# Wide pick for two tiles, and rows for five tiles fetched by SyncE, in a DLRM tower on one core

## The reference

```
e = jnp.stack([tbl_0[ids[:, 0]], tbl_1[ids[:, 1]], ..., tbl_26[ids[:, 26]]], axis=1)   # (2048, 27, 128)
interactions = jnp.einsum('bfd,bgd->bfg', e, e)
flat_interactions = interactions[:, _TRIU_I, _TRIU_J]                                   # (2048, 351)
z = jnp.concatenate([e.reshape(B, -1), flat_interactions], axis=1)
h = jnp.concatenate([z, dense_ctx], axis=1)                                             # (2048, 3823)
h = jnp.maximum(h @ W_top1 + b_top1, 0.0)                                               # 512
h = jnp.maximum(h @ W_top2 + b_top2, 0.0)                                               # 256
y = h @ W_top3                                                                          # (2048, 1)
```

## Time and profile before

| | us |
|---|---|
| median of 3 runs | 558.83 (558.7 to 559.23) |
| the profiled execution | 559.26 |
| its span, first to last instruction | 557.5 |
| outside the span | 1.76 |
| TensorE matmuls busy | 522.9 (94%) |
| GpSimd busy | 399.2 (72%) |
| ScalarE busy | 255.6 (46%) |
| VectorE busy | 243.9 (44%) |

### The profile page before, as it was taken

One profiled execution on the slowest core, in us unless ns is written; L12 is line 12 of the kernel. 1 busy time (PEld: TensorE's weight loads), 2 busy tenths in 40 slices (PEclk: granted clock), 3 DMA queues, 4 the chain that ended last, 5 costly groups with the idle time before them and its releaser, 6 DMA issues.

```text
span 557.5 us, 12647 instructions
## 1 busy us (share of the span) xinstructions
PE 522.9 (94%) x4420; PEld 429.9 (77%) x4420; DVE 243.9 (44%) x491; ACT 255.6 (46%) x488; POOL 399.2 (72%) x419
## 2 busy tenths in 40 slices
PE   0769889999999999999999999999999999999996
PEld 0547668878788788888888888888888888888884
DVE  3563533436254352534435253443525344352544
ACT  3674545353353535435353543535354353533542
POOL 6777777777777777777777777777777777777600
PEclk9998999999999999999999999999999999999999
DMA  6784321212112112211212121221212122111100
GB/s 171 257 256 130 110 54 57 57 54 60 53 56 59 55 54 56 60 54 57 59 54 59 54 59 54 58 61 55 59 54 59 53 57 60 55 53 54 53 2 1
DMA packets 27041, 38.80 MB, mean 70 GB/s; under 512 B 12455, under 2 KB 16504, under 8 KB 26978
## 3 DMA queue, kind: packets, MB, share of 16 engines
q0 software_dynamic: 13280, 27.22, 17.6%
q1 hardware_dynamic: 13698, 10.77, 6.7%
HBM read 37.96 MB, written 0.01 MB: 68 GB/s over the span
## 4 chain that ended last, share of the span: by engine, by line
PE 72%; POOL 17%; issue 6%; DMA 3%; ACT 1%; DVE 0%; DVEq 0%; ACTq 0%; POOLq 0%
POOL gathered L320 17%; PE p_hid L668 17%; PE p_hid L670 16%; PE p_hid L669 16%; PE p_prod L735 10%; PE p_group L638 7%; DMA gathered<-tbl_dram,idx 3%; PE p_group L626 1%; PE p_group L625 1%; PE p_hid_t L700 1%; PE p_group L655 1%; DMA idx<-ids_dram 0%; ACT emb L351 0%; PE p_hid L735 0%; PE p_hid_t L735 0%
## 5 line engine op out<-in xcount | busy, mean ns | idle before, releaser
L320 POOL DMA_INDIRECT gathered<-tbl_dram,idx x415 | 399.0, 961 | 128.5 <-issue 118.9
L668 PE MATMUL p_hid<-w_high,emb_high 128*128 128x512 f32 x432 | 183.6, 425 | 0.0
L670 PE MATMUL p_hid<-w_high,emb_low 128*128 128x512 f32 x432 | 171.0, 396 | 0.0
L669 PE MATMUL p_hid<-w_low,emb_high 128*128 128x512 f32 x432 | 169.7, 393 | 0.0
L469 DVE TENSOR_TENSOR emb_low<-p_group,emb_high 128x384 fp32r<-128x384 f32 x144 | 80.3, 558 | 195.3 <-ACT emb L351 194.8
L344 ACT ACTIVATE emb_high<-p_group 128x384 fp32r<-128x384 f32 x144 | 70.7, 491 | 161.3 <-PE p_group L638 145.3
L351 ACT ACTIVATE emb<-p_group 128x384 f32<-128x384 f32 x144 | 125.4, 871 | 0.0
L638 PE MATMUL p_group<-identity,gathered 128*128 128x128 f32 x415 | 73.2, 284 | 28.8 <-DMA gathered<-tbl_dram,idx 28.8
L670 PEld LDWEIGHTS p_hid<-w_high,emb_low 128*128 128x128 f32 x432 | 81.7, 189 | 19.4
L669 PEld LDWEIGHTS p_hid<-w_low,emb_high 128*128 128x128 f32 x432 | 82.5, 191 | 12.9
L668 PEld LDWEIGHTS p_hid<-w_high,emb_high 128*128 128x128 f32 x432 | 82.1, 190 | 12.4
(11 more groups left out here) (73 smaller groups left out, 358.6 us busy)
## 6 DMA issues: line engine op xcount, KB each, us to landing
fetched<-tbl_dram SPq DMA_DIRECT2D x512, 0.5 KB
w_stage<-w_dense_dram SPq DMA_DIRECT2D x27, 256.0 KB, 3.6
gathered<-tbl_dram,idx POOLq DMA_INDIRECT x415, 2.5
pick_ids<-ids_rows_dram SPq DMA_DIRECT2D x13, 62.5 KB
w_stage<-w_pairs_dram SPq DMA_DIRECT2D x3, 252.0 KB
w_stage<-w_dram SPq DMA_DIRECT2D x2, 256.0 KB, 3.8
w_stage<-tbl_dram SPq DMA_DIRECT2D x2, 250.0 KB
ctx_sb<-ctx_rows_dram SPq DMA_DIRECT2D x16, 13.5 KB
```

What stands on the lines that cost most here:

```text
L320: pool.indirect_dma_start(gathered[:, slot, k, :], None, tables[f], bass.IndirectOffsetOnAxis(ap=idx[:, t, f:f + 1], axis=0),).then_inc(gr ...
L668: nc.tensor.matmul(dst, high, w_high, start=start, stop=False)
L669: nc.tensor.matmul(dst, high, w_low, start=False, stop=False)
L670: return nc.tensor.matmul(dst, low, w_high, start=False, stop=stop)
```

## The change

The pick is made for two tiles at once. In the even tiles 2 to 12 VectorE makes the 0/1 matrices for the tile's own 128 samples behind `layer3` in the entry of group 4, and those of the next tile's samples in the entry of group 5, into one tensor with 256 columns. TensorE makes 16 matmuls of 256 columns, which fill the third and the fourth place of the bank. ScalarE copies the fourth place to `next_high` and to the next tile's `emb`, VectorE subtracts to `next_low`, and the next tile takes feature 26 from there. In tile 14, as in tiles 0, 1 and 15, it is gathered.

SyncE fetches feature 25 for tiles 4, 6, 9, 11 and 14. It takes the row numbers from SBUF, 32 at a time, and starts when the last weight's load is issued; it no longer does anything else in between. The loads of the context and of the pick's row numbers go out from ScalarE's queue, in the entries of groups 6 and 7 of the tile before. There are five staging slots for the weights. The room that the gathers' descriptors get is 2048 bytes per partition instead of 4096. `y` has 16 columns instead of 128, and the products' first row isn't brought into rows any more.

```diff
-    WIDE = NF + WRAP
-    STAGES = 4
+    WIDE = NF + WRAP - 1
+    STAGES = 5
...
+    PICK_TO = TILES - 2
...
-    picked_t = ids_rows.rearrange("(t b) -> t b", b=P)
+    picked_t = ids_rows.rearrange("(t b) -> t b", b=2 * P)
...
-    FETCH_TILES = [5, 8, 11, 14]
-    FETCH_PARTS = [0, 48, 96, P]
+    FETCH_TILES = [4, 6, 9, 11, 14]
     FETCH_ROWS = tables[FETCHED].shape[0]
-    LOADED = 16
+    LOADED = 32
...
     def picked_in(t):
-        return PICK_FROM <= t < LAST
-
-    def gathers_in(t, g):
-        return FEATS - (g == GROUPS - 1) * (picked_in(t) + (t in FETCH_TILES))
+        return PICK_FROM <= t < PICK_TO
+
+    def picks_start(t):
+        return picked_in(t) and t % 2 == 0
+
+    def picked_before(t):
+        return picked_in(t) and t % 2 == 1
+
+    def gathered_feats(t, g):
+        if g < GROUPS - 1:
+            return range(FEATS)
+        return [k for k in range(FEATS) if not (g * FEATS + k == PICKED and picked_in(t))
+                and not (g * FEATS + k == FETCHED and t in FETCH_TILES)]
...
-            pick = later("pick", [PICK_ROWS, PICK_CHUNKS, P], F32R)
-            pick_ids = [later(f"pick_ids_{k}", [PICK_ROWS, P], I32) for k in range(2)]
+            pick = later("pick", [PICK_ROWS, PICK_CHUNKS, 2 * P], F32R)
+            pick_ids = later("pick_ids", [PICK_ROWS, 2 * P], I32)
...
-        y = sb("y", [P, P])
-        y_rows = sb("y_rows", [TILES, P])
+        y = sb("y", [P, TILES])
...
+        def next_bank_of(t):
+            return p_group[ORDER.index((t, GROUPS - 1)) % 2][:, FEATS, :]
+
+        def feats_in(t, g):
+            return FEATS - 1 if g == GROUPS - 1 and picked_before(t) else FEATS
...
-            return bass.AP(products, ROWS_Q + first * (ROWS_Q + 1),
+            return bass.AP(products, first * (ROWS_Q + 1),
                            [[WIDE * ROWS_Q, P], [ROWS_Q + 1, rows], [ROWS_Q, DELTAS]])
...
+            def fetch_rows(n, b):
 
                 t = FETCH_TILES[n]
-                if part == 0 and n >= 2:
+                if b == 0 and n >= 2:
                     sp.wait_ge(group_transposed, FETCH_TILES[n - 2] * GROUPS + GROUPS)
-                for b in range(FETCH_PARTS[part], FETCH_PARTS[part + 1], LOADED):
-                    at = t * P + b
-                    _, rows = nc.values_load_multi_w_load_instructions(
-                        fetch_ids[at:at + LOADED].unsqueeze(0), engines=[mybir.EngineType.SP], min_val=0, max_val=FETCH_ROWS - 1,
-                        skip_runtime_bounds_check_because="ids are row numbers of the table")
-                    for k in range(LOADED):
-                        sp.dma_start(fetched[b + k:b + k + 1, n % 2, :], tables[FETCHED][bass.ds(rows[k], 1), :]).then_inc(
-                            rows_fetched[n % 2], 16)
-
-            def load_pick_ids(t):
-                wait(sp, pick_done, t - PICK_FROM - 1)
-                sp.dma_start(pick_ids[t % 2][:], picked_t[t].partition_broadcast(PICK_ROWS)).then_inc(
-                    pick_ids_loaded[t % 2], 16)
+                _, rows = nc.values_load_multi_w_load_instructions(
+                    fetch_ids_sb[t:t + 1, b:b + LOADED], engines=[mybir.EngineType.SP], min_val=0, max_val=FETCH_ROWS - 1,
+                    skip_runtime_bounds_check_because="ids are row numbers of the table")
+                for k in range(LOADED):
+                    sp.dma_start(fetched[b + k:b + k + 1, n % 2, :], tables[FETCHED][bass.ds(rows[k], 1), :]).then_inc(
+                        rows_fetched[n % 2], 16)
 
...
+            sp.dma_start(fetch_ids_sb[:], fetch_ids.rearrange("(t b) -> t b", b=P)).then_inc(fetch_ids_loaded, 16)
...
-            sp.wait_ge(w_low_done, len(STAGED))
-            for t in range(PICK_FROM, TILES):
-                load_ctx(t)
-                if t < LAST:
-                    load_pick_ids(t)
-                if (t - 2) // 3 < len(FETCH_TILES):
-                    fetch_rows((t - 2) // 3, (t - 2) % 3)
+            sp.wait_ge(fetch_ids_loaded, 16)
+            for n in range(len(FETCH_TILES)):
+                for b in range(0, P, LOADED):
+                    fetch_rows(n, b)
...
-                    for k in range(gathers_in(t, g)):
+                    for k in gathered_feats(t, g):
                         f = g * FEATS + k
...
+            def load_ctx(t):
+                act.wait_ge(ctx_used, t - 1)
+                act.dma_start(ctx_sb[:, t % 2, :], ctx_t[:, t, :]).then_inc(ctx_loaded[t % 2], 16)
+
+            def load_pick_ids(t):
+                act.wait_ge(w_low_done, len(STAGED))
+                wait(act, pick_done, t - PICK_FROM)
+                act.dma_start(pick_ids[:], picked_t[t // 2].partition_broadcast(PICK_ROWS)).then_inc(pick_ids_loaded, 16)
...
+                n = feats_in(t, g)
                 wait(act, group_used, s - SPLIT + 1)
-                nc.scalar.activation(emb_high[:, s % SPLIT, :, :], bank_of(t, g),
+                nc.scalar.activation(emb_high[:, s % SPLIT, 0:n, :], bank_of(t, g)[:, 0:n, :],
...
+            def copy_next(t):
+
+                if t > PICK_FROM:
+                    act.wait_ge(group_used, t * GROUPS)
+                nc.scalar.activation(next_high[:], next_bank_of(t), ACT.Copy).then_inc(next_high_done, 1)
+                act.wait_ge(round_done, t * ROUNDS)
+                nc.scalar.activation(emb[(t + 1) % 2][:, :, PICKED], next_bank_of(t), ACT.Copy).then_inc(next_copied, 1)
...
-                nc.scalar.activation(emb[t % 2][:, :, f0:f0 + FEATS].rearrange("p b f -> p f b"),
-                                     bank_of(t, g), ACT.Copy).then_inc(group_copied, 1)
+                n = feats_in(t, g)
+                nc.scalar.activation(emb[t % 2][:, :, f0:f0 + n].rearrange("p b f -> p f b"),
+                                     bank_of(t, g)[:, 0:n, :], ACT.Copy).then_inc(group_copied, 1)
...
                 else:
                     copy_high(t, g)
                     copy_whole(t, g)
+                if g == GROUPS - 1 and picks_start(t):
+                    copy_next(t)
...
+                if n == 6 and 2 <= t + 1 < TILES:
+                    load_ctx(t + 1)
+                if n == 7 and picks_start(t + 1):
+                    load_pick_ids(t + 1)
...
-                nc.vector.tensor_tensor(emb_low[:, s % SPLIT, :, :], bank_of(t, g),
-                                        emb_high_f32[:, s % SPLIT, :, :], ALU.subtract).then_inc(group_low_done, 1)
+                if g == GROUPS - 1 and picks_start(t):
+                    dve.wait_ge(next_high_done, (t - PICK_FROM) // 2 + 1)
+                    dve.wait_ge(next_copied, (t - PICK_FROM) // 2 + 1)
+                    nc.vector.tensor_tensor(next_low[:], next_bank_of(t), next_high[:].bitcast(F32),
+                                            ALU.subtract).then_inc(next_low_done, 1)
+                n = feats_in(t, g)
+                nc.vector.tensor_tensor(emb_low[:, s % SPLIT, 0:n, :], bank_of(t, g)[:, 0:n, :],
+                                        emb_high_f32[:, s % SPLIT, 0:n, :], ALU.subtract).then_inc(group_low_done, 1)
...
-                nc.vector.transpose(products[:, 0:NF, :], prod[:]).then_inc(rows_done, 1)
-                nc.vector.transpose(products[:, NF:WIDE, :], prod[:, 0:WRAP, :]).then_inc(rows_done, 1)
+                nc.vector.transpose(products[:, 0:NF - 1, :], prod[:, 1:NF, :]).then_inc(rows_done, 1)
+                nc.vector.transpose(products[:, NF - 1:WIDE, :], prod[:, 0:WRAP, :]).then_inc(rows_done, 1)
...
-            def make_pick(t):
-
-                dve.wait_ge(pick_ids_loaded[t % 2], ((t - PICK_FROM) // 2 + 1) * 16)
-                dve.wait_ge(w_low_done, len(STAGED))
-                wait(dve, pick_used, t - PICK_FROM)
+            def make_pick(t, half):
+
+                if half == 0:
+                    dve.wait_ge(pick_ids_loaded, ((t - PICK_FROM) // 2 + 1) * 16)
+                    wait(dve, pick_used, (t - PICK_FROM) // 2)
+                columns = slice(half * P, (half + 1) * P)
                 rows = table_row_sb[:].unsqueeze(2).broadcast_to([PICK_ROWS, PICK_CHUNKS, P])
-                ids_b = pick_ids[t % 2][:].unsqueeze(1).broadcast_to([PICK_ROWS, PICK_CHUNKS, P])
-                nc.vector.tensor_tensor(pick[:], ids_b, rows, ALU.is_equal).then_inc(pick_done, 1)
+                ids_b = pick_ids[:, columns].unsqueeze(1).broadcast_to([PICK_ROWS, PICK_CHUNKS, P])
+                nc.vector.tensor_tensor(pick[:, :, columns], ids_b, rows, ALU.is_equal).then_inc(pick_done, 1)
...
-            nc.vector.memset(y[:], 0.0).then_inc(zeroed, 1)
-            dve.wait_ge(zeroed, 3)
+            dve.wait_ge(zeroed, 2)
...
-                if n == 4 and PICK_FROM <= t < LAST:
-                    make_pick(t)
+                if n in (4, 5) and picks_start(t):
+                    make_pick(t, n - 4)
...
-                pe.wait_ge(pick_done, t - PICK_FROM + 1)
+                pe.wait_ge(pick_done, t - PICK_FROM + 2)
...
-                if g == GROUPS - 1 and picked_in(t):
```

(18 more changed lines are left out.)

25 lines of the change are left out of this document (15 added, 10 removed).

## The result

The changed kernel takes 555.71 us (median of six runs, 553.15 to 557.81), the kernel before 560.11 in the six runs beside it: a ratio of 0.9912, with a 95% interval of 0.9884 to 0.9939. It is 0.9% faster, clear of the 0.2% that a measurement can tell. The forecast was 558.2 against 558.83, 0.1% faster. The profiled run took 556.2 us with a span of 554.4, against 559.26 and 557.5. Where a set holds runs in a slower state of the chip, the ratio compares the undisturbed runs alone and the medians take all, so a ratio need not be the quotient of the two medians.

What follows compares the result with a forecast made beforehand. GpSimd's gathers were to be the bound from tile 2 to group 1 of tile 15: span 557.5 - 4.3 + 3.6 = 556.8, profiled 558.6, forecast 558.2 us against a median of 558.83; 8-in-10 range 553.5 to 561.2.

Steps and rivals of the forecast that it cites:

- The 4.3 us of slack: TensorE's lag behind the gather at group 1 of tile 15: no saving on TensorE can bring more than 4.3 us.
- Rival D: TensorE's wide matmuls cost double, so it saves only 1.6 us and stays the bound: 557.2 us, chance 0.03.
- 11.1 summed: TensorE's work saved: 9.5 us from six wide picks and 1.58 from tile 14 without a pick.
- the first half: First of two VectorE comparisons in each even tile: holds a GpSimd gather, losing 0.70 us per tile.
- The second half: Second comparison in each even tile, behind the pairs' subtraction: the gather behind the held one loses 0.4 us.
- the clock: GpSimd's gathers from tile 2 to group 1 of tile 15: 6.6 us held against 3.0, so +3.6 us.
- A: Comparisons miss the gathers: 555.7 us if only the second half misses, 551.5 if all miss; chance 0.28.
- The forecast's own range: Total held time beside comparisons of 5.5 to 8 us, so -1.8 to +0.7: 557.0 to 559.5 us.
- B: Each comparison starts as a gather ends, both halves held in full, 9.7 us against 3.0: 561.2 us, chance 0.15.
- C: Smaller descriptor room makes GpSimd wait for landings, gaps between gathers over 0.31 us: 563 us and more, chance 0.05.
- What hides the rest: Copies for the next tile, moved loads and SyncE's fetches stay hidden behind other work and cost nothing.
- The start-up's +-0.7: Fifth weight stage in tiles 0 and 1 shifts which gathers meet VectorE's weight subtractions: +-0.7 us.

Runs made afterwards that it cites:

- the control: The changed kernel run once more, nothing altered, beside two of its variants: 556.98 us against 559.73 for the kernel before, ratio 0.9941.

## Why the prediction was right in part, and which step failed

**Right: the bound and what a saving can bring.** The 4.3 us of slack in group 1 of tile 15 were the whole gain on TensorE, 4.20 measured. Matmuls of 256 columns stand 0.119 apart as predicted: in tile 8 the pick's 16 run from 302.80 to the transposes at 304.70:

```profile
302.80 0.28 PE L666 MATMUL p_group<-pick,table_high 125*128 125x256 f32 x1
...
304.70 0.38 PE L679 MATMUL p_group<-identity,gathered 128*128 128x128 f32 x2
```

That is 1.90 us. Rival D is out. From the transposes of group 1 of tile 2 to those of group 1 of tile 15, TensorE took 425.5 us with 1.9 of waits for gathers before, and 421.1 with 8.1 after: 10.6 us of work saved, for 11.1 summed. What was not gained went into waits. Over the whole span these grew by 8.8 us, for about 11 foreseen, and the last one stands at group 1 of tile 15.

**Failed: "the first half should cost what it cost there: mean of 0.61, 0.58, 0.82, 0.80 = 0.70".** This term was mis-sized. Measured is 0.27: nothing in tiles 2, 4, 6 and 8, 1.05 in tile 10, 0.58 in tile 12. The reason given, that TensorE's wait fixes the place, holds in part: in tiles 2 to 8 the comparison started 0.03 to 0.04 us behind a gather, not 0.3 to 0.5 ahead of one. The prediction had put the load of the row numbers among the edits that cost nothing because it costs ScalarE's queue little. It had not asked which transfer would be under way at the same time. That load made one gather in each pair land 0.4 to 1.2 us later, the subtraction of line 558 came over a gather's start and held it, the comparison then stood just behind a start, and a delay became a gain. That the load decides is shown by the run with the early load, in which the mean is 0.69 in tiles 4 to 12; that it works through the subtraction is read from the traces. The changed kernel in tile 10, GpSimd and VectorE, shows how thin the margin is:

```profile
362.87 1.22 DVE L585 TENSOR_TENSOR pick<-pick_ids,table_row_sb 125x1024 fp32r<-125x1024 int32 x1
362.93 1.99 POOL L330 DMA_INDIRECT gathered<-tbl_dram,idx  x1 [0.30 <-issue]
```

It starts 0.06 us earlier than the gather, and the gather loses 1.05.

**The second half**: 0.4 predicted, 0.27 measured and 0.35 in the run with the early load; the working was sound. So six times 0.54 = 3.27 were held, not 6.6, and the clock came 0.97 later, not 3.6. These 2.6 us are nearly all of the difference between 556.8 and 554.4 of span.

**Rivals.** The median, 555.71, is A's first figure, 555.7, but in part by luck: A's figure is 3.1 us under 558.83, and the kernel before had a median of 560.11 in the six runs beside the changed one, 4.4 us above the changed kernel's. The profiles, 3.1 us apart, fit A's sum. Still it is not A as written: it was the first half that missed in four tiles of six, and the second that was held. The forecast's own range, 557.0 to 559.5, was missed. B, both halves held in full, is out: 3.27 us were held, not 9.7. C is out: no gap between two gathers in tiles 2 to 15 is over 0.32 us.

**Who holds whom.** The Trainium skill, page "SBUF — State Buffer", section "SBUF: two separate sides", says that whoever starts first blocks the other for its whole instruction. The trace agrees when VectorE starts first. When the gather does, VectorE is not blocked for the gather's 0.94 us: the comparison at 170.56, started 0.03 into a gather, takes 1.23 us, where 1.21 to 1.22 is usual. It is delayed a little where both start together. The longest such delay is in tile 13 of the kernel before:

```profile
431.99 1.29 DVE L543 TENSOR_TENSOR pick<-pick_ids,table_row_sb 125x1024 fp32r<-125x1024 int32 x1
...
432.03 0.94 POOL L320 DMA_INDIRECT gathered<-tbl_dram,idx  x1 [0.30 <-issue]
```

Here the comparison is 0.04 us ahead and the gather is not held; at 0.06 ahead, above, it is held in full. The edge lies between the two.

**What hides the rest** held: no wait for the fetched rows is in the trace, nor for the next tile's bank. SyncE's fetches:

```profile
62.76 335.45 SPq L293 DMA_DIRECT2D fetched<-tbl_dram  x640
```

0.52 us a row, 67 a tile, for 69 foreseen. The start-up's +-0.7 came out at +0.43. The last gather started at 528.53, not at 530.6, as less was held, and is still 1.86 us ahead of TensorE's need.

## What to carry to other kernels

Before costing a saving, find the place behind which nothing waits any more and read the slack there; more than that slack no saving off the bound can bring, and what it touches on the new bound comes off. A cost that depends on the place of one instruction against another's period (0.03 us behind a start costs nothing, 0.06 ahead costs 1 us) is not to be forecast from a mean of tiles with another traffic: bound it from nothing to full, list every DMA that the change puts near the transfer that fixes the place and every instruction between that place and yours that can hold a gather, and where it can be had, remove the dependence altogether, here by one operand in PSUM. Measure such a kernel's variants beside the kernel before on the same chip, since a chip may have quite another bound.

## What the runs showed of the hardware

- On the ordinary chips a load of 125 rows of 1 KB on ScalarE's queue, issued between 0.6 us ahead of a gather and 0.8 us behind it, made it land 2.8 to 3.9 us after its issue, not 2.4 to 2.6; issued 13 to 14 us ahead, or 1.4 us behind (tile 10 with the row numbers in PSUM, 2.43), it did nothing.
- A gather started beside a VectorE instruction with two SBUF operands ends 0.82 us behind it (1.05 us lost at worst, for a start 0.06 us behind the comparison's; nothing for 0.04); beside the same instruction with one operand in PSUM it takes 0.94.
- A copy by VectorE from SBUF to SBUF (0.49 us, 351 numbers a partition) holds a gather too, 0.27 us in tile 2 of the control, again to 0.82 us behind its end.
- VectorE's comparison takes 1.21 to 1.22 us, and 1.23 to 1.29 where a gather starts within 0.04 us of it.
- A hold sets the gathers to VectorE: the next gather starts 1.12 us behind the end of the instruction that held the one before, and the later ones follow every 1.25 us.
- Several short VectorE instructions in close order can hold a gather as one long one does (it took 1.52 us).
- On some chips the same kernel took 702.6 and not 559 to 560 us, with a granted TensorE clock of 0.89 to 0.93 and engines idle for up to 12 us with no releaser in the profile. The cause is open.
